# A relation pass of a graph network kernel: sums by target and relation before the relation weights, instead of rows already multiplied by them

## The reference

```python
msg = x[src] @ rel_w[edge_type]
agg = segment_sum(msg, dst, 3125)
h = relu(agg + x @ self_loop_w.T) + x
x = layernorm(h)
```

## Time and profile before

| what | value |
|---|---|
| three runs, median | 4224.59 us (4211.87 to 4230.94) |
| the profiled execution | 4214.86 us, span 4213.1 us |
| TensorE busy, mean granted clock | 2946.0 us (70%), 0.863 |
| VectorE busy | 3186.2 us (76%) |
| ScalarE, GpSimd busy | 1371.8 us (33%), 1440.3 us (34%) |
| relation table, relation pass | 2597.8 to 2690.4 us, 2690.4 to 3344.9 us |

### The profile page before, as it was taken

How to read it: one execution, slowest core, us unless ns; L and a number is a source line. 1 busy time by engine, 2 the same in 40 slices (tenths; PEclk the granted TensorE clock), 3 DMA queues, 4 the chain that set the end, 5 groups by cost and what they waited for, 6 DMA issues and landing times. The chain is left out here.

```text
span 4213.1 us, 81525 instructions
## 1 busy us (share of the span) xinstructions
PE 2946.0 (70%) x27806; PEld 2295.3 (54%) x27806; DVE 3186.2 (76%) x7528; ACT 1371.8 (33%) x2613; POOL 1440.3 (34%) x1177
## 2 busy tenths in 40 slices
PE   0078888885077077076599985588888669949995
PEld 0055555553022022022599983388888569939995
DVE  7877778774898898899577763377777589958886
ACT  0034444542054054044499962233333200000000
POOL 0044545543577676776000000266666100000000
PEclk9988889886599599599699995599999789979997
DMA  8745566564487286287477630111111034313331
GB/s 319 320 138 161 165 181 185 166 164 156 135 286 228 73 290 225 69 288 224 142 219 218 217 115 13 61 24 24 25 24 24 9 86 108 105 31 91 92 90 41
DMA packets 405936, 582.74 MB, mean 138 GB/s; under 512 B 75350, under 2 KB 288938, under 8 KB 405156
## 3 DMA queue, kind: packets, MB, share of 16 engines
q1 hardware_dynamic: 359267, 449.19, 35.5%
q0 software_dynamic: 37056, 66.39, 5.5%
q10 hardware_dynamic: 9216, 62.01, 3.6%
HBM read 336.54 MB, written 234.26 MB: 135 GB/s over the span
## 5 line engine op out<-in xcount | busy, mean ns | idle before, releaser
L1123 PE MATMUL psum<-a_probs,z 128*65 128x512 f32 (+1 forms) x1050 | 446.9, 559 | 144.6 <-DVE a_probs L1056 144.5
L483 POOL DMA_INDIRECT slots<-h,idx x256 | 439.6, 1717 | 253.7 <-DMA h<-recs 183.2
L863 POOL DMA_INDIRECT slots<-bc_rec,idx x400 | 386.9, 967 | 390.0 <-ACT bc_rec L823 290.8
L1359 DVE TENSOR_SCALAR rp_hot_src<-rp_key_rows,lane 128x384 bf16<-128x384 f16 x1440 | 356.1, 317 | 156.4 <-issue 66.4
L1091 ACT ACTIVATE a_tops<-a_tops,a_s_low 128x1024 f32<-128x1024 f32 (+2 forms) x300 | 284.0, 947 | 567.9 <-DVE a_tops L1047 566.6
L1321 POOL DMA_INDIRECT rp_rows<-rel_rows,slot_rel x360 | 377.2, 1048 | 211.6 <-PE psum L1626 86.2
L1592 PE MATMUL psum<-rel_pieces,rp_hot_src 128*128 128x192 bf16 x4320 | 405.2, 248 | 61.5 <-issue 41.5
L1592 PEld LDWEIGHTS psum<-rel_pieces,rp_hot_src 128*128 128x128 bf16 x4320 | 357.3, 99 | 83.5 <-issue 58.1
L1123 PEld LDWEIGHTS psum<-a_probs,z 128*65 128x65 f32 x1050 | 121.9, 138 | 470.1 <-DVE a_probs L1056 301.0
L1047 DVE SCALAR_TENSOR_TENSOR a_tops<-table,a_s_rest,big 128x1024 f32<-128x1024 f32 (+2 forms) x300 | 306.7, 1022 | 32.5 <-DMA big<-shift_rows 32.5
L1056 DVE SCALAR_TENSOR_TENSOR a_probs<-a_tops,a_counts 128x1024 f32<-128x1024 f32 (+2 forms) x300 | 288.1, 962 | 1.0 <-issue 0.7
(11 more groups left out here) (462 smaller groups left out, 6528.0 us busy)
## 6 DMA issues: line engine op xcount, KB each, us to landing
a_counts<-edge_counts SPq DMA_DIRECT2D x150, 512.0 KB
slots<-big ACTq DMA_DIRECT2D x60, 1005.0 KB
ep_rec<-slots SPq DMA_DIRECT2D x60, 1005.0 KB, 5.6
edge_counts<-bc_counts SPq DMA_DIRECT2D x12, 3125.0 KB
hot_rows<-ep_hot_src SPq DMA_DIRECT2D x300, 96.0 KB, 4.9
sp_hot_src<-hot_rows SPq DMA_DIRECT2D x300, 96.0 KB, 1.9
sq_hot_src<-hot_rows SPq DMA_DIRECT2D x300, 96.0 KB, 1.9
recs<-bc_rec SPq DMA_DIRECT2D x100, 268.0 KB
```

Source lines behind the costliest of these rows:

```text
L483: pool.indirect_dma_start(k.slots, bass.IndirectOffsetOnAxis(k.idx[:, at:at + 1], 0), self.rows[y][:, t, :], None).then_inc(self.scattered ...
L863: pool.indirect_dma_start(k.slots, bass.IndirectOffsetOnAxis(k.idx[:, first + t:first + t + 1], 0), rec[:, j, t, :], None).then_inc(scatte ...
L1123: last = nc.tensor.matmul(sums[:, a:b], k.z[:, s, 0:D + 1], probs[:, a:b], start=s == 0, stop=True, skip_group_check=True)
L1359: last = v.tensor_scalar(hot_src[:, n % HOT_SLOTS, rel, :], key_rows[:, n % 2, :], k.lane[:, rel:rel + 1], None, ALU.is_equal)
```

## The change

1. The relation table is gone. `node_mlp` splits `x` into three bf16 pieces and writes `x_rows`, 64 columns a node.
2. A new `relation_pass` takes the relations' place. SyncE loads the stored source one-hots of all 300 chunks. One product of 192 columns looks a slot up. VectorE makes one one-hot of 696 columns a slot: 8 relations x 87 targets, from a key that the setup puts into the record. The looked-up row is now the *weights* and the one-hot the moving side, so that the sums come out as features x (relation, target), 696 columns in two banks (512 and 184). The first two pieces fill all 128 output rows in one product; the third piece fills 64, the upper half for a unit's first slot, the lower for its second. Units are two slots, groups are three units; the third pieces of a group come after its first ones.
3. When a triple (75 slots) is summed, ScalarE copies the sums to SBUF, and one triple later TensorE multiplies them by the relation weights (held twice, for both halves), 24 float32 products, summed over relations in PSUM. The last triple's follow at the end.
4. Left-over slots of the relations: the row is turned, multiplied by all relations, masked by type, reduced.
5. In all passes the next left record is loaded as soon as the left message is made; VectorE takes its number after three banks, not six.
6. Records have one more number (540 instead of 536 bytes); describing a chunk in the edge pass costs one VectorE instruction less.

```diff
-REC = H + 6
+REC = H + 7
@@ setup
+                parts = [p for name, source in weight_sources(d).items() for p in weight_parts(k, name, source)]
@@ edge_slots
+                chain.link(v.scalar_tensor_tensor(meta[:, 0:ET, 6], d_bin[:, :], -float(SPAN), dst[:, :], ALU.mult, ALU.add))
+                chain.link(v.scalar_tensor_tensor(meta[:, 0:ET, 6], meta[:, 0:ET, 5], float(SPAN), meta[:, 0:ET, 6],
+                                                  ALU.mult, ALU.add))
@@ edge_pass, SyncE, left-over loop
-                    sp.wait_ge(left_sum, i * LEFT_BANKS + LEFT_BANKS)
+                    sp.wait_ge(left_hot, i + 1)
+                    sp.wait_ge(left_msg, i + 1)
@@ edge_pass, describe
-                    v.scalar_tensor_tensor(k.slot_rel[:, at], got[:, :, H + 3], float(RELS), got[:, :, H + 5],
-                                           ALU.mult, ALU.add)
-                    chain.link(v.tensor_tensor(k.slot_lo[:, at], got[:, :, H + 3], first, ALU.subtract))
-                    v.scalar_tensor_tensor(k.slot_key[:, at], got[:, :, H + 5], float(P), k.slot_lo[:, at],
-                                           ALU.mult, ALU.add).then_inc(described, 1)
+                    v.tensor_tensor(k.slot_key[:, at], got[:, :, H + 6], got[:, :, H], ALU.add)
+                    v.tensor_tensor(k.slot_lo[:, at], got[:, :, H + 3], first, ALU.subtract).then_inc(described, 1)
@@ edge_pass, VectorE, left-over loop
-                        if b == LEFT_BANKS - 1:
+                        if b == 3:
@@ relation_pass, new
+    SRC_SLOTS, HOT_SLOTS, MSG_UNITS, GROUP_UNITS, PAIR = 8, 18, 9, 3, 2
+    KEYS, ROW = RELS * SPAN, 3 * D
+    PARTS, REST = ((0, BANK), (BANK, KEYS)), KEYS - BANK
...
+                def hot_target(q):
+                    if q >= HOT_SLOTS:
+                        dve.wait_ge(added, GROUP_OF[UNIT_OF[q - HOT_SLOTS]] + 1)
+                    v.tensor_scalar(hot_dst[:, q % HOT_SLOTS, :], ramp[:, :], k.slot_key[:, q:q + 1], None, ALU.is_equal)\
+                        .then_inc(dst_made, 1)
...
+                def take_rows(u):
+                    n = len(UNITS[u])
+                    act.wait_ge(looked_up, u + 1)
+                    if u >= MSG_UNITS:
+                        act.wait_ge(added, GROUP_OF[u - MSG_UNITS] + 1)
+                    nc.scalar.activation(msg[:, u % MSG_UNITS, 0:n, :], row_bank(u, n), ACT.Copy).then_inc(rows_taken, 1)
...
+                def look_up(u):
+                    if u >= 2:
+                        pe.wait_ge(rows_taken, u - 1)
+                    for i, q in enumerate(UNITS[u]):
+                        c, s = q // SLOTS, q % SLOTS
+                        pe.wait_ge(hot_io[c % SRC_SLOTS], 16 * (c // SRC_SLOTS + 1))
+                        last = nc.tensor.matmul(row_bank(u, PAIR)[:, i, :], hot_src[:, c % SRC_SLOTS, s * P:(s + 1) * P],
+                                                pieces[:, c % NT, :, :].rearrange("p a f -> p (a f)"), start=i == 0, stop=True,
+                                                skip_group_check=True)
+                    last.then_inc(looked_up, 1)
...
+                def add_first(u):
+                    pe.wait_ge(rows_taken, u + 1)
+                    for i, q in enumerate(UNITS[u]):
+                        pe.wait_ge(dst_made, q + 1)
+                        s = q % SLOTS
+                        if q % PER_TRIPLE < SLOTS and q >= PER_TRIPLE:
+                            pe.wait_ge(sums_taken, (q // PER_TRIPLE - 1) * 2 + s // 2 + 1)
+                        for part, (a, b) in enumerate(PARTS):
+                            nc.tensor.matmul(sum_bank(s, part), msg[:, u % MSG_UNITS, i, 0:2 * D],
+                                             hot_dst[:, q % HOT_SLOTS, a:b], start=starts_bank(q, part), stop=True,
+                                             skip_group_check=True)
...
+                def add_rest(g):
+                    for u in GROUPS[g]:
+                        for part, (a, b) in enumerate(PARTS):
+                            for i, q in enumerate(UNITS[u]):
+                                last = nc.tensor.matmul(sum_bank(q % SLOTS, part)[i * D:(i + 1) * D, :],
+                                                        msg[:, u % MSG_UNITS, i, 2 * D:3 * D], hot_dst[:, q % HOT_SLOTS, a:b],
+                                                        start=False, stop=True, skip_group_check=True)
+                    last.then_inc(added, 1)
...
+                def multiply(j):
+                    pe.wait_ge(sums_taken, (j + 1) * 2)
+                    if j >= 1:
+                        pe.wait_ge(evacuated, j)
+                    for s in range(SLOTS):
+                        for r in range(RELS):
+                            last = nc.tensor.matmul(out_bank(s), by_relation[:, j % 2, s, r * SPAN:(r + 1) * SPAN],
+                                                    weights[:, r * D:(r + 1) * D], start=r == 0, stop=True,
+                                                    skip_group_check=True)
+                    last.then_inc(multiplied, 1)
...
+                look_up(0)
+                for g, units in enumerate(GROUPS):
+                    for u in units:
+                        if u + 1 < len(UNITS):
+                            look_up(u + 1)
+                        add_first(u)
+                    add_rest(g)
+                    j = g // PER_GROUPS
+                    if g % PER_GROUPS == PER_GROUPS - 1 and j >= 1:
+                        multiply(j - 1)
+                multiply(NTRIPLE - 1)
@@ node_mlp, after the layer norm
+        split_pieces(k, chain, k.x[:, :, :], piece_parts(pieces, D), k.big[:, :, 0:D])
+    phase.tables = [(k.x_rows.rearrange("(t p) f -> p t f", p=P), k.x[:, :, :])]
@@ program
-        with nc.sbuf_tensor("rel_pieces", [P, looked_up, RELS, 3 * D], BF16) as pieces:
-            with nc.sbuf_tensor("rel_rest", [P, LOOKED_UP, RELS * D], FP32) as k.rel_rest:
-                relation_table(k, pieces)
-            edge_pass(k, "rp", "relations", pieces, k.rel_rows, D, D)
+        with nc.sbuf_tensor("node_pieces", [P, NT, 3, D], BF16) as pieces:
+            node_mlp(k, pieces)
+            relation_pass(k, pieces)
```

More of the change, by code:

```diff
@@ L104, in weight_sources, with weight_parts @@
     return at
+def weight_parts(k, name, source):
+    if name == "Wrel":
+        return [(k.weight[name][a:a + D, :], source) for a in (0, D)]
+    return [(k.weight[name][:, :], source)]
 @contextmanager
@@ L152, in bin_parts, with node_parts @@
             ((0, first, edge), (edge - first, edge, end)) if stop > start]
-def by_lookup(c):
-    return c % NT % NB % 2 == 0
-LOOKED_UP = NB // 2 + 1
+def node_parts(b):
+    first, end = b * SPAN, min(b * SPAN + SPAN, N)
+    edge = min(end, (first // TN + 1) * TN)
+    return [(start - first, stop - start, start // TN, start % TN) for start, stop in
+            ((first, edge), (edge, end)) if stop > start]
 class Program:
```

498 lines of the change are left out of this document (282 added, 216 removed).

## The result

| | before | after |
|---|---|---|
| median, same chip | 4218.2 us (4207.8 to 4230.9, 4 runs) | 4040.3 us (4033.5 to 4056.6, 4 runs) |
| profiled execution | 4214.9 us, span 4213.1 | 4056.6 us, span 4054.9 |
| relation table, from x to the pass | 92.6 us | 12.9 us |
| loop of the relation pass | 619 us | 562.9 us |
| its tail | 35.5 us | 26.7 us |

The ratio of the medians is 0.958, interval 0.954 to 0.9625: faster. 4090 was forecast; 4040.3 lies 5 us under the low end of the range. The profiled execution is the slowest of its four, so the medians differ by 178 us and the two profiled executions by 158.

What follows compares the result with a forecast made beforehand. TensorE's products were taken to bound the relation loop. Table -76, loop -34, tail -6, other passes -17, setup and records +4 sum to -129 from 4214.9 us: 4086, stated as 4090, range 4045 to 4220.

Steps and rivals of the forecast that it cites:

- R1: Relation loop: third-piece halves run one after another, 0.293 us each, kernel 4198 us; chance 0.11.
- R2: Relation loop: halves one after another, weights loaded only when the array is idle, kernel 4288 us; chance 0.09.
- R3: Relation loop: TensorE's 88 us of idle time stay, loop 648 us, kernel 4149 us; chance 0.08.
- R4: Relation loop: halves overlap, but mode changes empty the array and half weights load late, kernel 4203 us; chance 0.05.
- R5: Relation loop: no holes, with mode changes, late weights and ScalarE wait at zero, kernel 4028 us; chance 0.04.
- A: Relation table: 92.6 us replaced by splitting x and a 64-column table, 16.6 us; -76 us.
- C: Tail of the relation pass: 35.5 us before, new left-over work less savings and a shorter fetch end; -6 us.
- D: Left record loaded early in the three other passes, 5.6 us each; -17 us.
- B: Relation loop: 619 us becomes 585, from 517 of products plus waits, mode changes and start; -34 us.
- Terms (1) and (2): Relation loop: 312 mode switches at 0.08 us, 25 us; 912 pairs with weights perhaps late at 0.02, 18 us.
- Term (3): Relation loop: TensorE waits for ScalarE's copy, short by 0.05 us in 304 units; 15 us, between 0 and 36.
- Term (4): Start of the relation loop: first look-up 2.6 us, half clock 4, first triple's sums 3; 10 us.

Runs made afterwards that it cites:

- e1: Changed kernel with the second slot's third piece put into the same upper half as the first's: 4178.8 us, ratio 0.9915.
- e8: Changed kernel plus 360 indirect GpSimd fetches of 128 rows that nobody uses, in the relation loop: 4180.9 us, ratio 0.9874, loop 674.3 us.
- the group runs: Changed kernel with one, four or five units per group instead of three: 4118.6, 3887.0 (another chip) and 4038.9 us; loop 617.3, 542.6 and 537.8 us.
- e9: Kernel before with its 360 GpSimd fetches replaced by plain SyncE transfers of other rows: 4085.9 us, ratio 0.9687, loop 494.7 us.
- e6: Kernel before with only the left record loaded early: 3933.0 us, ratio 0.9949.
- e11: Changed kernel plus 360 unused plain GpSimd transfers of 128 rows in the relation loop: 4058.0 us, ratio 0.9599, loop 550.8 us.
- e13: Changed kernel plus 360 unused indirect GpSimd fetches of 16 rows each: 4178.8 us, ratio 0.9894, loop 677.8 us.
- e15: Changed kernel plus 360 unused indirect GpSimd fetches, each with its own wait: 3895.0 us, ratio 0.9855, loop 550.8 us.
- e5: Changed kernel with the left record loaded late again in all four passes: 3922.3 us.
- e16: Changed kernel plus 240 unused indirect GpSimd fetches in 120 pairs: 3901.4 us, ratio 0.9871, loop 550.7 us.
- e7: Kernel before with 2 instead of 8 buffers for fetched rows in the relation pass: 3959.8 us, ratio 1.0011.
- e2: Changed kernel with the third-piece products ordered slot outside, column part inside: 4044.1 us, ratio 0.9595.

## Why the prediction was wrong, step by step

**The side and the mechanism were right.** The table's products went, TensorE bounds the loop at clock 1.00, the halves run at once, neither VectorE nor ScalarE took over, and the old loop's idle time did not survive. R1 and R2 fell with e1; R3 (holes stay) is what e8 shows, where the indirect fetches stayed, though its 88 us of holes are too few for e8's 124; R4 fell with the group runs, 34 us for all changes of mode where it had 51 and 109 more for weights. R5, the rival that was given 0.04, was nearest in number: 4028 us. Its mechanism, terms (1) to (3) at zero, did not hold for the changes of mode; the parts A, C and D made up for them.

**The step that failed is B, in the terms that stand beside the products.** The twelve triples at 43.1 us are 517 us. The measured loop is 562.9, so 46 us remain where 68 were put.
- Terms (1) and (2), changes of mode and weights not in place, 43 us: the groups show 0.21 to 0.22 us each, 156 times, **33 to 35**. Little is left for weights not in place: with these and 517 and term (4) the sum is 557 to 559 of the 562.9.
- Term (3), the wait for ScalarE, 15 us: **0**. I had the copy's way 0.05 us longer than its cover. In the rows above it ends 0.07 us before the product that reads it, and over the loop TensorE's products wait 1.4 us for ScalarE's sums and 0.3 us for its messages.
- Term (4), the start, 10 us: **6.4**. The first look-up comes 2.4 us after the pass begins (2611.26), the first group, most of it at half clock, takes 6.0 us, 2.6 more than a later one, and the first triple's sums hold TensorE for 1.4.

**The other terms.** A: 79.8 instead of 76; the splitting was right (6.8 us for 6.7), but from the write to the pass is 6.1 us, not the near pass's 9.9. C: 8.8 instead of 6, because the last fetch's end shrank by 8.0 and not by the 3 taken. (The prediction's 10.6 counts from that fetch's end; from its start it is the 13.0 above.) I had 0 to -6 and took half; e9, without the 360 fetches but with the old tail, goes from the last fetch (3200.04) to the next stage (3206.53) in 6.5 us. In the other profiles this end takes 7.0 to 13.7 us where GpSimd had made 360 transfers in the pass (before, e6 to e8, e11, e13, e15) and 5.0 to 6.1 where it had made fewer or none, so the slow end comes with the transfers, and the full -6 was right. D: 23.4 instead of 17. I had 5.6 for each of three passes, read off the near pass, and near and far gave 5.8 and 6.0 here (8.2 and 5.8 by e5). The miss is in the edge pass, 11.6: its record was worth 8 or more, and the shorter description, of which I had said under E that ScalarE hides it, some 4. E: within the spread of the program's start.

**The range.** The terms missed by 22 + 4 + 3 + 6 us, all in one direction, less 6 in E. That makes 29 us against the profiled execution, still inside the range; the other 16 is that execution's place among its four. The range took the lower ends of the terms (1) to (3) as a rival of their own with 4 chances in 100, although nothing in the rows spoke for a ScalarE wait but a difference of 0.05 us between two sums of eight durations. A term so small beside the errors of its parts stands for as much below as above.

**What I did not see at all** is where the gain comes from. Without its fetches the old loop is 494.7 us (e9) and the new one 550.5: as work for TensorE the change is 56 us dearer. The forecast's -34 for the loop was a sum of new products against a loop with 88 us of holes. Of the stall at its start the prediction said that it goes "with those fetches or with the long instruction stream". It is the fetches, and for the later holes too. On a chip where they do no harm (old loop 510) the change loses 40 us in the loop, wins 80 at the table and some 23 in the other passes, and ends near 60.

## What to carry to other kernels

Before a restructured loop is credited with idle time of the old one, ask what operation goes with it, and take that operation out of the old loop and put it into the new one: here two such runs showed that the fetches, not the algebra, made the loop faster, on the chips where it became faster at all. A row that names a releaser long done, or "issue" on several engines at once, is a hint to look at what another engine is doing, and a kernel is worth comparing on more than one chip when such rows make up its gain. Two products of 64 output rows each, put into different halves, took the time of one here, and each change into and out of them cost 0.22 us, so gather as many as buffers allow.

## What the runs showed of the hardware that was not expected

- **Indirect fetches by GpSimd can hold up engines that have nothing to do with them.** 360 of them cost 124 us, of 16 rows as of 128, a row of 21 alone 24 us of it; 360 plain transfers by GpSimd or SyncE and 360 iotas cost nothing, and 120 single fetches 1.5 us. What carries it is not settled, since the waits have no releaser in the record. That closeness decides and not number is what the rows of 21, three and one suggest; e15 and e16, which were to test it, met a chip without the effect. On such chips, by the same mark, the part of the program in which GpSimd writes records out indirectly is also some 150 us shorter (the first attention scores are written at 897.6 us in e7, at 1050.4 before); that part was not experimented on.
- **There are two levels for this kernel, by the chip**: before took 4213 to 4231 us in five comparisons and 3952 and 3956 in two on other chips, and the change was worth 155 to 178 us on the former and, by the two nearest kernels timed there, 57 to 61 on the latter.
- **Half products overlap whatever their order**: twelve take 1.01 us in different halves, with neighbours in the same half too, and 1.89 when all share one, 1.9 times. The Trainium skill's TensorE: Matmul & The Clock Gate, "Part 3: Packing small matmuls", has 2.38 times for three column tiles. Here, by two and with streams of 512 and 184 columns, the whole factor is had but for 0.13 us of each row of twelve.
- **The products of the two halves did not start in the kernel's order**: written as 512, 184, 512, 184 columns, the two of 512 started 7 ns apart and the two of 184 after them (e2).
